# A selective-scan block with its MLP on one core: every engine's order is rewritten, and three kinds of startup transfer move behind chunk 0's rows of C

## The reference

```
x = x + s6(layernorm(x))          # selective scan, 16 states per channel
x = x + quantized_linear(layernorm(x))

s6: xp = x @ x_proj_w.T            # 64 columns for delta, 16 for B, 16 for C
    delta = softplus(xp[:64] @ dt_proj_w.T + dt_proj_b)
    h[t] = exp(delta*A) * h[t-1] + delta * B[t] * x[t]    # for each of 512 x 16 states
    y[t] = sum over the 16 states of h * C[t]  + x * D
quantized_linear: rows of x rounded to 8 bits by their own scale, times 8-bit weights,
    times both scales, plus bias
```

## Time and profile before

| | |
|---|---|
| runs shown | 2790.3, 2790.7, 2793.21 us |
| profiled execution | 2791.34 us, its span 2789.6 us, mean granted PE clock 0.996 |
| busy share of the span | PE 98%, DVE 97%, ACT 97%, POOL 96% |
| DMA | 344 MB, mean 123 GB/s |

### The profile page before, as it was taken

The page is one execution under the profiler, slowest core; times in us unless marked ns, Lnnn a source line. Parts: engine busy times, 40 slices in busy tenths (PEclk is TensorE's granted clock), DMA queues, the critical chain, the costliest instruction groups (busy, mean ns, idle before and its releaser), DMA issues.

```text
span 2789.6 us, 59136 instructions
## 1 busy us (share of the span) xinstructions
PE 2746.0 (98%) x22516; PEld 2516.2 (90%) x22516; DVE 2711.7 (97%) x2801; ACT 2694.8 (97%) x4927; POOL 2689.7 (96%) x980
## 2 busy tenths in 40 slices
PE   7999999999999999999999999999999999999998
PEld 6899999899998999998999989999989999999987
DVE  6999999999999999999999999999999999999987
ACT  7999999999999999999999999999999999999994
POOL 4899999999999999999999999999999999999998
PEclk9999999999999999999999999999999999999999
DMA  5245454465454554444654545545446544464442
GB/s 199 78 125 130 124 127 117 112 149 124 109 139 105 138 130 123 128 121 109 153 122 107 139 104 139 130 126 125 121 109 149 123 109 137 104 140 115 122 122 54
DMA packets 271653, 344.33 MB, mean 123 GB/s; under 512 B 174917, under 2 KB 174917, under 8 KB 251018
## 3 DMA queue, kind: packets, MB, share of 16 engines
q1 hardware_dynamic: 250538, 275.54, 34.8%
q0 software_dynamic: 20832, 65.02, 13.1%
HBM read 253.60 MB, written 103.16 MB: 128 GB/s over the span
## 4 chain that ended last, share of the span: by engine, by line
PE 36%; POOL 21%; ACT 15%; DMA 12%; issue 12%; DVE 4%; SPq 1%; POOLq 0%; ACTq 0%; DVEq 0%
POOL A L546 18%; PE Y L799 11%; PE PB L774 8%; DMA out<-C 8%; PE PB L777 8%; ACT A L611 7%; ACT DB L632 3%; DVE A L932 3%; DMA CB<-c_rows 2%; ACT C L661 2%; PE PM L858 2%; POOL C L563 2%; PE PM L839 2%; PE PM L899 1%; PE Y L795 1%
## 5 line engine op out<-in xcount | busy, mean ns | idle before, releaser
L546 POOL TENSOR_TENSOR A<-A,CB 128x2048 f32<-128x2048 f32 x511 | 2336.3, 4602 | 58.9 <-ACT CAR L618 29.0
L932 DVE TENSOR_TENSOR_SCAN A<-A,CAR,PB 128x512 f32<-128x512 f32 x1536 | 1832.7, 1259 | 13.2 <-PE PB L777 8.3
L611 ACT ACTIVATE A<-DEL,an 128x512 f32<-128x512 f32 x2048 | 1311.7, 712 | 5.5 <-PE Y L799 5.1
L799 PE MATMUL Y<-idf,A 128*128 128x128 f32 x8192 | 1091.5, 273 | 0.0
L799 PEld LDWEIGHTS Y<-idf,A 128*128 128x128 f32 x8192 | 938.4, 141 | 34.2 <-issue 16.4
L632 ACT ACTIVATE DB<-XN,BC 128x512 f32<-128x512 f32 x1344 | 897.4, 712 | 7.8 <-DVE XN L962 5.2
L777 PE MATMUL PB<-idf,DB 128*128 128x128 f32 x5376 | 763.6, 274 | 19.2 <-DVE A L932 12.0
L774 PEld LDWEIGHTS PB<-DG,XN 128*128 128x128 f32 x5632 | 687.0, 192 | 87.0 <-issue 79.1
L774 PE MATMUL PB<-DG,XN 128*128 128x128 f32 x5632 | 729.6, 277 | 1.2 <-DVE A L932 0.6
L777 PEld LDWEIGHTS PB<-idf,DB 128*128 128x128 f32 x5376 | 619.5, 142 | 37.3 <-DVE A L932 12.4
L932 DVE TENSOR_TENSOR_SCAN A<-A,PB 128x512 f32<-128x512 f32 x512 | 584.3, 1200 | 23.6 <-PE PB L774 13.3
(11 more groups left out here) (92 smaller groups left out, 1371.1 us busy)
## 6 DMA issues: line engine op xcount, KB each, us to landing
CB<-c_rows SPq DMA_DIRECT2D x128, 1024.0 KB, 6.1
DG<-b_diag SPq DMA_DIRECT2D x192, 256.0 KB, 3.0
X<-in_x SPq DMA_DIRECT2D x31, 1024.0 KB, 7.8
out<-X SPq DMA_DIRECT2D x31, 1024.0 KB, 5.1
out<-bias_rows POOLq DMA_DIRECT2D x31, 1024.0 KB, 8.1
out<-C POOLq DMA_DIRECT2D x31, 1024.0 KB, 12.1
b_diag<-DG SPq DMA_DIRECT2D x2, 1536.0 KB, 11.7
b_diag<-BC SPq DMA_DIRECT2D x192, 2.0 KB, 2.5
```

Source lines behind the costliest of these rows:

```text
L546: gp.tensor_tensor(A[s % NA][:, :, :], A[s % NA][:, :, :], CB[:, s % (4 * NG), :].unsqueeze(1).broadcast_to([128, KB, L]), ALU.mult).then_ ...
L611: act.activation(A[s % NA][:, g, :], DEL[k % 2][:, g, :], ACT.Exp, scale=an[:, g, n:n + 1])\
L799: i = pe.matmul(Y[j][:, g * 128:(g + 1) * 128], A[s % NA][:, g, j * 128:(j + 1) * 128], idf[:, :], is_transpose=True, start=False, stop=(n ...
L932: dve.tensor_tensor_scan(A[s % NA][:, g, :], A[s % NA][:, g, :], PB[(4 * s + g) % NPB][:, :], init, ALU.mult, ALU.add).then_inc(s_scan, 1)
```

## The change

1. All three order tables get new numbers. FIRST now covers the whole of chunk 0 on most tasks, where it used to end after the first units.
2. On SP, only one blank array is written ahead of the ordered tasks. A new task `late` sends the rest by key: 0 is the first half of wq, 1 the second blank array, 2 the second half of wq, 3 wsb, bib and the bias rows. x of chunk 2 is loaded by the ordered `load`.
3. Both halves of wq are staged in C, one after the other, so `late` 2 waits for the first cast, and `weights` becomes two tasks. ACT's wait in `act_b` for the casts goes.
4. The second blank comes out of DG slot 3, which POOL zeroes with one more memset; s_zd becomes a pair of semaphores, and the load into slot 3 waits for the second blank's end.
5. In the middle chunks the order of SP changes so: `load` of x, formerly right ahead of `turn`, now follows `load_c` 0 of the chunk two before; `turn` now stands ahead of `load_c` 3; `store_c` of the next chunk now stands behind the loads of its diagonals 1 to 3. On POOL, `scale_p`, `shift0` and `xn_p` stand behind unit 15, `add_c` behind unit 0, `ascale` behind unit 6 (it was 5), and `add_b` right ahead of `centre`.

```diff
 PLACES = {
...
+        "late": (-300, -290, 200, 250),
-        "load": (-2254,),
-        "load_c": (91, 545, 545, 706),
-        "load_g": (-320, -16, -2, 187, 679, 680),
+        "load": (-1750,),
+        "load_c": (230, 412, 805, 942),
+        "load_g": (-115, 13, 13, 164, 884, 885),
...
-        "stats0": (-2032, -2028, -2022, -1604),
+        "stats0": (-1250, -1240, -1230, -1220),
-        "store_c": (-276,),
-        "store_g": (-322,),
+        "store_c": (229,),
+        "store_g": (-117,),
...
-        "weights": (-475,),
+        "weights": (-100, 300),
...
-        s_zd = sem("s_zd")
+        s_zd = [sem(f"s_zd{i}") for i in range(2)]
...
             def later(p):
-                if p >= 3:
+                if p >= 2:
                     load(p)
...
             def store_g(p):
                 sp.wait_ge(s_bce, p + 1)
-                if p == 0:
-                    sp.wait_ge(s_zd, 32)
+                if p <= 1:
+                    sp.wait_ge(s_zd[p], 16)
...
                 if e >= NR:
                     sp.wait_ge(s_tb, 4 * diag_unit(e - NR) + 4)
+                elif e == NR - 1:
+                    sp.wait_ge(s_zd[1], 16)
...
             load(1)
-            sp.wait_ge(s_zero, 1)
-            for i in range(2):
-                sp.dma_start(dg[i, 0:128 * W].rearrange("(p n w) -> p n w", p=128, n=NDG),
-                             DG[:, 0, :, :].rearrange("p j c -> p (j c)").unsqueeze(1).broadcast_to([128, NDG, T * 128]))\
-                  .then_inc(s_zd, 16)
-            for h, stage in enumerate((C, DB[2])):
-                sp.dma_start(stage[:, :, :].rearrange("p t d -> p (t d)").bitcast(int64).rearrange("p (k o) -> p k o", k=2),
-                             wq[256 * h:256 * h + 256, :].rearrange("(k p) o -> p k o", p=128)).then_inc(s_w2, 16)
-            sp.dma_start(wsb[:, :], ws.partition_broadcast(128)).then_inc(s_w2, 16)
-            sp.dma_start(bib[:, :], bias.partition_broadcast(128)).then_inc(s_w2, 16)
-            sp.dma_start(b4[:, :], bias.partition_broadcast(4)).then_inc(s_b4, 16)
-            load(2)
+            sp.wait_ge(s_zero, 2)
+            blank(0, 0)
+
+            def late(p, i):
+                if p:
+                    return
+                if i == 1:
+                    blank(1, NR - 1)
+                elif i < 3:
+                    h = i // 2
+                    if h:
+                        sp.wait_ge(s_wb, 1)
+                    sp.dma_start(C[:, :, :].rearrange("p t d -> p (t d)").bitcast(int64).rearrange("p (k o) -> p k o", k=2),
+                                 wq[256 * h:256 * h + 256, :].rearrange("(k p) o -> p k o", p=128)).then_inc(s_w2, 16)
+                else:
+                    sp.dma_start(wsb[:, :], ws.partition_broadcast(128)).then_inc(s_w3, 16)
+                    sp.dma_start(bib[:, :], bias.partition_broadcast(128)).then_inc(s_w3, 16)
+                    sp.dma_start(b4[:, :], bias.partition_broadcast(4)).then_inc(s_b4, 16)
...
             gp.memset(DG[:, 0, :, :], 0.0).then_inc(s_zero, 1)
+            gp.memset(DG[:, NR - 1, :, :], 0.0).then_inc(s_zero, 1)
...
-                    if m == 2:
-                        act.wait_ge(s_wb, 2)
...
-            def weights(p):
+            def weights(p, h):
                 if p:
                     return
-                dve.wait_ge(s_w2, 64)
-                for h, stage in enumerate((C, DB[2])):
...
+                dve.wait_ge(s_w2, 16 * (h + 1))
```

More of the change, by code:

```diff
@@ L23 @@
[L23 to L29, removed]
+        "aggr0": (-1180,),
+        "amax": (1157,),
+        "ascale": (1228,),
@@ L74 @@
-        "xn": (-783, -777, -767),
-        "xn_p": (-641,),
-        "xp_out": (-632,),
+        "q_mm": (1839, 1871, 1878, 1880),
+        "q_t": (155, 684, 752, 1722),
+        "qt_out": (1734, 1799, 1802, 1803),
+        "root": (1345,),
+        "rstd0": (-1060,),
+        "scale_a": (1812, 1896, 1918, 2013),
+        "scale_out": (20000, 20001, 20002, 20003),
+        "scale_p": (1890,),
+        "scales": (1178,),
+        "scan": (15, 65, 65, 65, 65, 101, 114, 114, 114, 114, 114, 114, 114, 114, 118, 128, 128, 128, 128,
@@ L94 @@
[L94 to L109, removed]
+        "act_b": (-29235, -29229, -28856, -28288, -27665, -26059, -24650, -21309, -20216, -19572, -15945,
+        -15945, -15945, -12040, -12040, -11768, -11767, -11284, -11284, -8129, -6817, -6759, -6118, -4314,
+        -3117, -2352, -119, -94, -62, -3, 9, 58, 58, 58, 66, 265, 361, 371, 561, 568, 576, 689),
+        "add_b": (1318,),
+        "add_c": (2152,),
@@ new lines @@
+        "dl_t": (-18780, -18099, -18099, -16168),
+        "du": (-1402, -1306, -1306, -1306),
+        "gather": (1117, 1117, 1125, 1126),
+        "inv": (1207,),
+        "late": (-12995, -12985, 100, 200),
+        "load": (16363,),
+        "load_c": (-34082, -7485, -6765, 435),
+        "load_g": (-30274, -17300, -16756, -4842, -4602, -852),
+        "log0": (-83651,),
+        "put_x": (1716,),
+        "q_mm": (1845, 1857, 1876, 1884),
+        "qt_out": (1759, 1765, 1773, 1773),
+        "root": (1498,),
@@ new lines @@
+        "shift0": (-88312,),
+        "square": (1117, 1184, 1319, 1329),
+        "stats0": (-56459, -46320, -38392, -34964),
+        "step": (1379,),
+        "store_c": (-44487,),
+        "store_g": (-39959,),
[9 rows of a table added]
+        "times_c": (-11758, -8632, -4412, -3209, -1284, -523, -412, 53, 86, 199, 227, 227, 227, 227, 294, 515),
+        "turn": (2007,),
+        "var1": (1363,),
+        "weights": (-100, 300),
+        "x_p": (-30660, -29608, -29608, -29603),
+        "x_t": (-49113, -39517, -31939, -31009),
@@ L117 @@
-        "add_b": (-985,),
+        "act_b": (-246, -245, -245, -245, -245, -103, -54, -33, -18, 92, 105, 154, 154, 154, 154, 157, 157,
+        320, 322, 505, 505, 569, 569, 569, 604, 604, 604, 604, 604, 604, 604, 604, 604, 1162, 1460, 1460,
+        1557, 1557, 1557, 1569, 6821, 7778),
+        "add_b": (-67304,),
         "add_c": (42071,),
[L119 to L126, removed]
+        "amax": (4676,),
+        "ascale": (3686,),
+        "centre": (45306, 15024, 17561, 19098),
+        "decay": (-142, -53, 41, 83, 83, 83, 85, 85, 151, 152, 210, 210, 210, 210, 214, 214, 267, 267, 267,
@@ L459, in put_last @@
                     sp.dma_start(of[p * L + j * 128:p * L + (j + 1) * 128, :], rows(p)[:, j, :]).then_inc(s_end, 16)
-            run(put_last=put_last, turn=lambda p, i: turn(p), load=lambda p, i: later(p), store_c=lambda p, i: store_c(p), load_c=load_c,
+            run(put_last=put_last, late=late, turn=lambda p, i: turn(p), load=lambda p, i: later(p), store_c=lambda p, i: store_c(p), load_c=load_c,
                 store_g=lambda p, i: store_g(p), load_g=load_g, put_x=lambda p, i: put_x(p))
```

146 lines of the change are left out of this document (82 added, 64 removed), and 48 rows, old and new, of tables (FIRST, LAST, PLACES).

## The result

The changed kernel takes 2775.1 us, the median of four runs (2773.16 to 2778.11), against 2790.5 (2787.25 to 2793.21) for the kernel before on the same chip: 15.4 us less, ratio 0.9945 with a 95% interval of 0.9930 to 0.9961. The forecast was 2781.7, with a range of 2774 to 2797. So direction and range held, and the size did not: 15.4 us where 9 had been worked out.

A forecast was written before the change was run, and what follows sets the result against it. It saw no engine leading in the middle, with PE's 0.26 us idle a chunk as the ceiling if PE's work is the floor. 2790.7 - 4.0 (start) - 3.5 (middle) - 1.5 (end) = 2781.7 us, range 2774 to 2797.

The forecast's parts named there:

- The memset, +0.5: Startup: the new POOL memset stands before the mask for the warm-up transposes and adds all its time, +0.5 us.
- The rows of C and the diagonals: Startup: c_rows land in 2.5 to 5 us, `load_c` 0 goes out at 24, first DG at 26.5, before use.
- ACT is late next: Chunk 0: ACT's carries become the late item, so POOL's first product stays at about 35 us; POOL gains 3.
- The start, -4.0: Startup gain, taken between PE's 3.5 and DVE's 5.5 us, less the memset's 0.5; bounds 0 and -9.
- Cost 0: Startup, late transfers: wq's second half goes out near 60 us for a cast near 76, at no cost.
- The middle, -3.5: 28 middle chunks: waits go, gaining half of PE's idle time of 7.3 us; bounds -7.3 and +7.
- The end, -1.5: Last chunk: DVE's waits of 1.09 and 1.27 us are spread, POOL waits about 1.3; bounds -3 and +2.
- Only the start moves: Rival: the middle stays as it is and only start and end gain, 2785 us; chance 0.2.
- ACT takes the gain of the start: Rival: the first chunk ends up bound by ACT and the rest loses a little, 2788 to 2791; chance 0.12.
- SP holds back the fourth group of C rows: Slower rival, middle chunks: `turn` ahead of `load_c` 3 makes POOL wait at unit 12, 2797 or 2811; chance 0.13.
- E + 1.5 + T: Middle chunks: when `load_c` 3 goes out, E being `centre`'s end and T `turn`'s hold on SP; landing 4.9 to 6.1 later.
- The clock rival: First 60 us: PE's slow-clock stretch may last longer, costing DVE 2 to 3 us once; about 3 on the sum.

The follow-up runs named there:

- f_small: The changed kernel with the second cast of weights moved later, behind the third scan of unit 10, and the new memset behind the mask: 2771.03 us.
- e_ahead: The changed kernel with the transfers sent ahead of the ordered tasks again, except wq's second half: 2776.08 us, ratio 0.9950 to before.
- r_start: The changed kernel's code and orders up to about 213 us (chunk 2), the orders of before from there on: 2789.19 us, ratio 0.9998.
- best: The changed kernel with f_small's two edits and `turn` behind `load_c` 3, except the turn of chunk 30: 2769.51 us, ratio 0.9921.
- g_turn: The changed kernel with `turn` moved behind `load_c` 3: 2785.2 us, ratio 0.9982.
- r_mid: The kernel before with the changed orders only from about 213 us to about 2400 us: 2782.54 us, ratio 0.9978.
- p_half: The kernel before with half of the quantised product left out, orders and waits unchanged: 2791.48 us in one run, against 2790.87 for before.
- m_inv: The kernel before with `inv` three scans later, `scales` two scans later and `ascale` behind one more POOL unit: 2790.81 us, ratio 1.0005.
- r_end: The kernel before with the changed orders from 2400 us on: 2787.52 us, ratio 0.9993.

## Why the prediction was right and where it failed

**The memset, +0.5: wrong, it is 0.** In the timelines of after and f_small the first real transpose is at 11.93 and 11.86 us, and over all kernels here it comes at 10.7 to 11.9 with the memset ahead and at 11.3 to 12.3 without. The prediction put it on the path because the warm-up had run right up to that transpose; but the transpose waits for XN, not for the warm-up.

**The rows of C and the diagonals: right.** 1.6 us to land (under the 2.5 to 5 given), `load_c` 0 at 22.0, first DG at 25.5.

**ACT is late next: right.** The carries of units 0, 1, 2 and 4 were put at 35, 44.5, 49.4 and 59; POOL's products start at 35.29, 44.57, 49.58 and 60.05, each on CAR. ACT works from 22.68 to 50.1 without any gap. It is also why e_ahead loses nothing.

**The start, -4.0: mis-sized, it is -1 to -2.5.** At chunk 1's first scan after is 1.6 us ahead of before and r_start 2.5, at chunk 4's after is 1.0 ahead; r_start's time of 0.0 does not count against this, since its switch took about 3 us. The 5.5 us at unit 2 came (41.14). The next stretch gave back 3.9: from unit 2's first scan to chunk 1's takes 75.71 us in after and 71.82 before. The failed step is "Cost 0" for the second half of wq. Its transfer was in time, but the cast itself took 2.83 us in a place where before had no cast. DVE's busy time in the stretch is 3.1 us longer and its idle time 0.8. f_small shows it by experiment: with the cast elsewhere the stretch is 71.68 us (72.42 in `best`), and the kernel is 4.1 us faster. f_small and `best` are 6.1 and 5.1 us ahead of before at chunk 1's first scan, so with this step seen -4.0 would have been a fair size, on the careful side.

Why the cast took four times as long can be read off the rows. Seven casts were issued into a running product of POOL, in after, r_start, g_turn, f_small, `best` and twice in e_ahead, and each ended 0.54 to 0.56 us after this product did: 85.39 after 84.84 in f_small, 86.19 after 85.65 in `best`, 40.53 after 39.97 in e_ahead. First e_ahead's cast, then POOL and DVE in `best`:

```profile
39.34 1.19 DVE L921 CAST wqb<-C 128x1024 bf16<-128x1024 int32 x1
```

```profile
76.61 9.04 POOL L601 TENSOR_TENSOR A<-A,CB 128x2048 f32<-128x2048 f32 x2 [2.22 <-ACT CAR L673]
```

```profile
84.51 1.68 DVE L965 CAST wqb<-C 128x1024 bf16<-128x1024 int32 x1
```

A cast beside an idle POOL takes 0.67 us. So the cast behaves as if it waited for the whole instruction that POOL has begun and then ran at its own speed. POOL pays as well: its two products from 76.96 take 9.47 us in after, beside the cast, and the same two 9.04 in f_small, where it comes later. The Trainium skill ("SBUF — State Buffer", Who interferes with whom) says that a cast on VectorE can enter a mode that uses the port pair shared with GpSimd, and that whoever comes first holds the pair for its whole instruction; the trace agrees, with 2.83 us against 0.67. The scans beside the same products are not held up: in after 22 in a row from 51.57 take 24.55 us, 1.12 each, and in the earlier trace rows 11 take 12.51, 1.14 each.

**The middle, -3.5: mis-sized, it is -10 to -12** in the traces (-11.9 between chunks 4 and 28, -10.6 in r_mid between 4 and 24), beyond its bound of -7.3. r_mid's time shows 6.6 us, with its second switch's 2.4 to 4.5 us inside. The failed step is "None of the engines gets more than its idle time back, and PE's is 0.26 x 28 = 7.3 us". PE's idle time is no ceiling, since a busy PE is not PE at its peak: in p_half PE is spared 3 us of work a chunk and the chunk stays at 85.2 us. e_ahead says the same from the other side: from 400 to 2400 us it has after's pace, 84.7 us a chunk, and PE is idle there for 10.1 us, as in before (10.0), while DVE's idle time fell from 20.2 to 12.4. The engine with the least idle time left is then DVE, with 0.84 us a chunk in this stretch, and half of it came back. That DVE's own pace is the next limit is argued from this and not shown by a run. The waits that were named did go (inv from 17.9 us to 1.1, out<-C from 13.9 to 1.4), yet m_inv shows that one such wait taken away by itself is worth nothing. What is shown is that the whole set of orders brings it; which edge of it does is open.

**The end, -1.5: about right.** r_end has -1.7, with an interval that holds 0, but the traces agree with one another: from chunk 28's first scan to the end r_end, e_ahead, f_small and `best` take 366.9 us each, and before 369.2, r_mid 369.4 and r_start 369.3, so -2.3 to -2.5. After's own trace shows only -0.3, because its chunk 28 took 85.5 us where these four take 83.7; what held it there is not known.

**The sum.** That the range held is luck in part: the middle came out beyond its bound, and the start fell short of its size the other way.

**The rivals.** "Only the start moves" is refuted, it was the other way round. "ACT takes the gain of the start" is refuted too: with the same order on ACT, f_small keeps 6.1 us at chunk 1's first scan, so it was the cast that took the gain and not ACT. "SP holds back the fourth group of C rows" has its mechanism in the trace and not its price. `turn` fell to 4.4 us in the median, against 7.2 in the earlier trace rows, though `add_b` had been issued about 4 us ahead of it, and still POOL waits before unit 12 in ten chunks. The longest such wait between 715 and 2068 us, on SP and then on POOL:

```profile
1363.95 5.82 SPq L474 DMA_TRANSPOSE C<-C  x1
1369.87 1.00 SPq L459 DMA_DIRECT2D DG<-b_diag  x2
1370.96 0.38 SPq L436 DMA_DIRECT2D CB<-c_rows  x1
```

```profile
1378.94 18.11 POOL L599 TENSOR_TENSOR A<-A,CB 128x2048 f32<-128x2048 f32 x4 [1.50 <-DMA CB<-c_rows]
```

`centre` ended at E = 1363.9. The load went out at E + 7.0, as the prediction's E + 1.5 + T has it (7.3), but it needed 7.8 us to land, not 4.9 to 6.1. The mis-sized term is this landing time: `load_c` 3 lands after 5.7 to 8.1 us in chunks 5 to 26 of after, 7.0 in the median, and it had needed 8.0 in the median in before too. POOL's waits in the sixteen chunks:

```profile
POOL A L599 <- DMA CB<-c_rows: 6.0, 10, 1.5
POOL A L599 <- ACT CAR L671: 0.2, 1, 0.2
```

Of the 6.0 us only 2.9, in five chunks, stand before unit 12 and belong to `turn`; the other 3.1 stand before unit 4, which `load_c` 1 feeds, and the prediction had no such wait. POOL paid for both out of waits that the new order had taken away (9.5 us on `inv` and 5.3 on CAR in this stretch before). What `turn` costs in the end is 1 to 3 us: between chunks 1 and 28 g_turn gains 3.2 us on after and `best` 1.0 on f_small. The clock rival is small: 0.91 against 0.93 in the first 100 us, and after, at 0.80 from 30 to 60 us, is no more than 0.7 to 0.9 us behind r_start and g_turn, at 0.94, though it began its units 1.0 to 1.3 us later than they did.

## What to carry to other kernels

Take the ceiling of a reordering from the idle time of the engine whose own pace the period approaches, not from the engine with the highest busy share; leaving out half of a suspect's side work is a cheap test. When a moved instruction is costed by a row, look at what ran beside it in that row: a cast that takes 0.7 us beside an idle POOL took 2.8 beside a working one. Before moving transfers out of the way, see what is late next: here moving them was worth nothing that the runs could tell. A table of marks, one for each chunk, shows which stretch really paid; it also shows what the experiment itself costs, as the switches between two orders did here.

## What the runs showed of the hardware

- A cast of 128x1024 from int32 to bf16 on DVE takes 0.67 us beside an idle POOL and 1.19, 1.68, 1.89, 2.83 and 3.03 us beside a running 128x2048 product of POOL, by how long that product still has to run.
- The transposing DMA holds SP for less when no 1 MB load has been issued right ahead of it (after, 4.4 us in the median), and for more when one has (before, 7.2, behind x; g_turn, 9.1, behind `load_c` 3). Times on SP and landing times, after and then g_turn:

```profile
L474 SPq DMA_TRANSPOSE C<-C x31: 3840/4400/6671, 181.3 to 2699.2; - x31
...
DMA to landing us min/median/max: 6.2/7.1/8.7
```

```profile
L474 SPq DMA_TRANSPOSE C<-C x31: 5237/9058/11038, 180.7 to 2711.8; - x31
...
DMA to landing us min/median/max: 7.3/11.4/13.5
```

- 32 KB behind 8 to 9 MB of earlier transfers land after 11.8 us (e_ahead) and 12.1 (before), behind about 4 MB after 1.6.
